# The recurrent stage of a four-layer graph kernel: 512 columns per matmul instead of 256, PSUM shared by two streams, straight-line code

## The chip, the cores and the metric

One core of a Trainium2 chip runs the whole program. The time is that of the device for one execution, in microseconds (us). The core has five engines that run side by side and meet at semaphores: TensorE (PE in the profile; PEld is its weight load), VectorE (DVE), ScalarE (ACT), GpSimd (POOL) and SyncE (SP, which issues the transfers between memory and SBUF). TensorE writes only to PSUM, which has 8 banks of 512 fp32 values in each of 128 partitions.

## The reference, cut to what matters

The input x is [128 graphs, 64 nodes, 256 features], and each of four layers computes `x = layernorm(x + layer(x))`. Layer 0 is a spectral convolution with attention and an MLP. Layer 1 is two graph convolutions followed by four small LSTMs, and it is the one that the change is in. Layer 2 is a graph convolution with two batch norms. Layer 3 is a masked attention. The part of layer 1 that matters here:

```python
def _lstm_last(Wih, Whh, bih, bhh, xs):          # xs [N, p, 256]
    bias = bih + bhh
    def step(carry, x_t):
        h, c = carry
        g = x_t @ Wih.T + h @ Whh.T + bias       # 1024 gate columns
        i, f, gg, o = jnp.split(g, 4, axis=-1)
        c = sigmoid(f) * c + sigmoid(i) * tanh(gg)
        h = sigmoid(o) * tanh(c)
        return ((h, c), None)
    ...                                          # h and c start at zero
for p in range(1, 5):                            # "skip" p
    nw = 64 // p
    wins = h[:, :nw * p, :].reshape(128 * nw, p, 256)
    last = _lstm_last(Wih[p-1], Whh[p-1], bih[p-1], bhh[p-1], wins)
    h = h.at[:, arange(nw) * p + p - 1, :].set(last)
```

For skip p there are 128 x (64 // p) windows, and each goes through p steps one after the other. In the first step h and c are zero, so neither Whh nor the forget gate is needed there. Skip p+1 reads what skip p has written.

## The kernel before, in words

The state `H` lies in SBUF with the 256 features on the partitions (two blocks of 128, `KD` = 2) and the 8192 tokens along the free side. Matrix products that must be exact to nearly fp32 are done by `exact_mm` (line 295): each operand is split into a rounded high part and a low rest (both fp32r), and three matmuls (high x high, low x high, high x low) accumulate. So a gate half (128 of the 1024 gate columns) costs 2 x 3 = 6 matmuls in a window's first step and 12 in a later one. A first step has three gates (36 matmuls), a later step four (96).

The recurrent stage (lines 1041 to 1252) runs two streams, s = 0 and 1 (`LS` = 2). Each takes a chunk of graphs so that a step has 256 columns (`COLS`): 4, 8, 12 and 16 graphs for skips 1 to 4 (for skip 3, 252 of the 256 columns hold data, and 84 in the last chunk of each stream, but all 256 are streamed). The order on each engine is: skip, turn, step j, stream. PE does one step of stream 0, then one of stream 1, and so on. Each stream has four PSUM banks of its own, one for each gate; a bank holds both halves of 256 columns (`gate_ps`, line 1112).

One step goes like this. PE waits for the split input `xin[s]` and for `hid_ready[s]` (the stream's previous step is wholly done), and does the gates in the order input, candidate, forget, output. ACT takes each gate out of PSUM with sigmoid or tanh (line 1155, two instructions per gate), and after the last gate takes the tanh of the cell (line 1160). DVE computes the cell (lines 1201 to 1207) and the new h (line 1212), and splits h into `hin[s]` (lines 1214 and 1216); in a window's last step it writes to `H` instead (line 1219). Then ACT and DVE split the input of the stream's next step (lines 1146 and 1189). While they do this, PE does the other stream's step.

The turns of a skip are a loop (`Fori`) whose last turn or two are written out. At the start of each skip, ACT and DVE split the new weights into the single weight buffer `w_r` (lines 1142 and 1180) and the inputs of both streams' first steps, which need the whole of the skip before. The raw weights come by DMA into staging areas in `H2`. Those of layer 2 are split at the start of the next stage (lines 1342 and 1369), whose first PE work is line 1407 and whose first DVE work is line 1377.

Of the kernel before, what the change touches and what calls it, by code (L numbers as in the profile page):

```python
# [121 lines left out]
def build_program(nc, ctx, t, out_rows):  # L122
# [23 lines left out]
    H2 = sb("H2", [P, KD, BATCH, NODES])  # L146
    Hflat = H[:].rearrange("p k b n -> p k (b n)")
    H2flat = H2[:].rearrange("p k b n -> p k (b n)")
# [42 lines left out]
    sm_inv = sb("sm_inv", [P, STREAMS, 2 * NJ])  # L191

# [47 lines left out]
    st = region(H2_words[:, 2 * 4096:])  # L240
    lstm_stage = [[st(KD, GATES * D), st(KD, GATES * D)] for _ in range(2)]
    l2r = region(H2_words[:, 2 * 4096:])
    l2_raw = [l2r(KD, HID2), l2r(MB, D)]
# [4 lines left out]
    W3_WORDS = 3 * KD * ATT3 + 2 * D  # L248

# [39 lines left out]
    def raw(v):  # L289

        return v.bitcast(F32)
# [15 lines left out]
    lstm_loaded = [sem(f"lstm_loaded{p}") for p in range(MAX_SKIP)]  # L307
    l2_loaded = sem("l2_loaded")
# [330 lines left out]
    with nc.Block() as block:  # L639

        @block.sync
        def _(sp):
# [19 lines left out]
            sp.dma_start(lstm_stage[0][0], t["wih"][0]).then_inc(lstm_loaded[0], 16)  # L662
# [270 lines left out]
    with nc.Block() as block:  # L933

        @block.sync
        def _(sp):
            for s in S:
                sp.dma_start(xg_t[s], rows_of_group(state0, s, 0)).then_inc(xg_loaded[s], 16)
            sp.dma_start(lstm_stage[1][0], t["wih"][1]).then_inc(lstm_loaded[1], 16)
            sp.dma_start(lstm_stage[1][1], t["whh"][1]).then_inc(lstm_loaded[1], 16)  # L940
# [101 lines left out]
    COLS = 256  # L1042
    lb = region(H2_words[:, 0:2 * 4096])
    gate = [lb(GATES, KD * COLS) for _ in range(LS)]
    cell = [lb(KD * COLS) for _ in range(LS)]
    hid = [lb(KD * COLS) for _ in range(LS)]
    lr = region(R[:])
    w_r = lr(2, 2, KD, GATES * D)
    xin = [lr(2, KD, COLS) for _ in range(LS)]
    hin = [lr(2, KD, COLS) for _ in range(LS)]  # L1050
    order = (0, 2, 1, 3)

    def gates_of(j):
        return [q for q in order if not (q == 1 and j == 0)]

    class Skip:

        def __init__(self, p):
            self.p = p  # L1060
            self.nw = NODES // p
            self.nb = COLS // self.nw
            self.turns = -(-BATCH // (self.nb * LS))
            self.nb_last = (BATCH - self.nb * LS * (self.turns - 1)) // LS
            self.per_turn = sum(len(gates_of(j)) for j in range(p))
            self.stage = lstm_stage[(p - 1) % 2]
            self.parts = [(w, k) for w in range(1 if p == 1 else 2) for k in range(KD)]
            self.gates_done, self.act_done = sems(f"gates_done{p}_", LS), sems(f"act_done{p}_", LS)
            self.x_hi, self.x_ready = sems(f"x_hi{p}_", LS), sems(f"x_ready{p}_", LS)
            self.cell_ready, self.tanh_ready = sems(f"cell_ready{p}_", LS), sems(f"tanh_ready{p}_", LS)  # L1070
            self.hid_ready, self.steps = sems(f"hid_ready{p}_", LS), sems(f"lstm_steps{p}_", LS)
            self.w_hi, self.w_ready = psem(f"w_hi{p}"), psem(f"w_ready{p}")

        def graphs(self, turn):
            return self.nb_last if isinstance(turn, int) and turn == self.turns - 1 else self.nb

        def window(self, turn, s, j):

            n = self.graphs(turn)
            last = isinstance(turn, int) and turn == self.turns - 1  # L1080
            first = (self.turns - 1) * LS * self.nb + s * n if last else (turn * LS + s) * self.nb
            return H[:, :, bass.ds(first, n), j:j + self.p * (self.nw - 1) + 1:self.p]

        def as_window(self, v, turn):

            n = self.graphs(turn)
            return v[:, :, 0:n * self.nw].rearrange("p k (b w) -> p k b w", b=n)

        def run(self, eng, step):

            looped = self.turns - 1 if self.nb_last == self.nb else self.turns - 2
            with eng.Fori(0, looped) as i:
                for j in range(self.p):
                    for s in range(LS):
                        step(i, j, s, (i, j + 1) if j < self.p - 1 else (i + 1, 0))
            for turn in range(looped, self.turns):
                for j in range(self.p):
                    for s in range(LS):
                        after = (turn + 1, 0) if turn < self.turns - 1 else None
                        step(turn, j, s, (turn, j + 1) if j < self.p - 1 else after)  # L1100

        def wait_for_all(self, eng):

            for s in range(LS):
                eng.wait_ge(self.hid_ready[s], self.turns * self.p + 1)

    skips = [Skip(p) for p in range(1, MAX_SKIP + 1)]

    def blocks_at(q, s):
        return blocks_of(gate[s][:, q, :])  # L1110

    def gate_ps(s, q, m):
        b = q * KD + m
        return ps[:, 4 * s + b // 2, (b % 2) * COLS:(b % 2 + 1) * COLS]

    with nc.Block() as block:

        @block.sync
        def _(sp):
            for skip in skips:  # L1120
                p, parts = skip.p, skip.parts
                if p in (1, 2):
                    sp.wait_ge(skip.w_ready, len(parts))
                    sp.dma_start(lstm_stage[(p + 1) % 2][0], t["wih"][p + 1]).then_inc(lstm_loaded[p + 1], 16)
                    sp.dma_start(lstm_stage[(p + 1) % 2][1], t["whh"][p + 1]).then_inc(lstm_loaded[p + 1], 16)
                if p == 3:
                    sp.wait_ge(skip.w_ready, len(parts))
                    sp.dma_start(l2_raw[0], t["L2W1"]).then_inc(l2_loaded, 16)
                    sp.dma_start(l2_raw[1], t["L2W2"]).then_inc(l2_loaded, 16)
                    for dst, name in ((Wq3, "Wq3"), (Wk3, "Wk3"), (Wv3, "Wv3"), (Wo3, "Wo3")):  # L1130
                        sp.dma_start(dst, t[name]).then_inc(l3_loaded, 16)
                    sp.dma_start(bo3, rows("bo3")).then_inc(l3_loaded, 16)

        @block.scalar
        def _(act):
            for skip in skips:
                p, parts = skip.p, skip.parts
                act.wait_ge(lstm_loaded[p - 1], 16 if p == 1 else 32)

                def split_weights(parts):  # L1140
                    for w, k in parts:
                        act.activation(w_r[:, 0, w, k, :], skip.stage[w][:, k, :], ACT.Copy).then_inc(skip.w_hi, 1)

                def split_x(s, turn, j):

                    act.activation(skip.as_window(xin[s][:, 0], turn), skip.window(turn, s, j), ACT.Copy)\  # L1146
                       .then_inc(skip.x_hi[s], 1)

                def step(turn, j, s, nxt):
                    done = sum(len(gates_of(jj)) for jj in range(j))  # L1150
                    act.wait_ge(skip.hid_ready[s], turn * p + j + 1)
                    for n, q in enumerate(gates_of(j)):
                        act.wait_ge(skip.gates_done[s], turn * skip.per_turn + done + n + 1)
                        for m in range(KD):
                            ins = act.activation(blocks_at(q, s)[:, m, :], gate_ps(s, q, m),  # L1155
                                                 ACT.Tanh if q == 2 else ACT.Sigmoid,
                                                 bias=lstm_bias[:, p - 1, 2 * q + m:2 * q + m + 1])
                        ins.then_inc(skip.act_done[s], 1)
                    act.wait_ge(skip.cell_ready[s], turn * p + j + 1)
                    act.activation(blocks_at(2, s), blocks_of(cell[s]), ACT.Tanh).then_inc(skip.tanh_ready[s], 1)  # L1160
                    if nxt:
                        split_x(s, *nxt)

                split_weights(parts[:KD])
                if p > 1:
                    skips[p - 2].wait_for_all(act)
                for s in range(LS):
                    split_x(s, 0, 0)
                split_weights(parts[KD:])
                skip.run(act, step)  # L1170

# [639 lines left out]
```

## Time and profile before

| what | value |
|---|---|
| median of 3 runs | 2538.29 us (2537.64 to 2539.34) |
| profiled execution, span from first to last instruction | 2536.9 us |
| PE busy | 2313.9 us, 91% |
| DVE busy | 1616.9 us, 64% |
| ACT busy | 1306.8 us, 52% |
| mean granted TensorE clock | 0.977 |
| recurrent stage, first to last matmul | about 904.3 to 1962.5 us |

The profile gives no time for its own execution other than the span. The median of the runs is 1.4 us above it, and that difference is taken as what lies around the span. Busy time on PE is the union of the matmul records, whose ends are modelled. A matmul's record is longer than its spacing from the next, so the spacing is read from counts over a busy stretch and not from the mean duration.

### The profile page before, as it was taken

The page shows a single profiled execution, that of the slowest core. Times are in us where ns is not written, and L with a number is a line of the kernel's source. Part 1 is how long each engine was busy: PE and PEld are TensorE (multiplying, and loading weights), DVE is VectorE, ACT ScalarE, POOL GpSimd, SP SyncE. Part 2 cuts the span into 40 slices and gives each one's busy share as a digit, 9 for nine tenths or more (in the row PEclk, how much of TensorE's full clock was granted, in tenths as well). Part 3 has the DMA queues.
Part 4 walks back from the last instruction along what each step waited for, and adds up shares of the span by engine and source line. Part 5 has one row for each costly group of instructions (what it writes and reads, how often), then busy time and mean ns, then how long its engine had stood idle before and what let it go on. Part 6 is the DMA issues. An engine that isn't in the chain of part 4 may idle for free. (4 is left out here: it accounts for less than half of the span.)

```text
span 2536.9 us, 48069 instructions
## 1 busy us (share of the span) xinstructions
PE 2313.9 (91%) x17943; PEld 2195.9 (87%) x17943; DVE 1616.9 (64%) x3379; ACT 1306.8 (52%) x2645; POOL 496.5 (20%) x937
## 2 busy tenths in 40 slices
PE   5989998999969999999999999999999897968887
PEld 4888888888869999999999999999999897956665
DVE  4898889888955544444444443444443787858887
ACT  1343344334423379755554444444443666957775
POOL 3334433433430000000000000000000221035554
PEclk9999999999989999999999999999999898989998
DMA  3010011011121100000000000000000331012111
GB/s 98 22 51 29 30 41 50 21 34 44 34 100 50 49 33 0 34 0 0 0 28 1 0 0 1 1 1 0 0 0 1 116 116 34 0 38 67 58 59 45
DMA packets 76385, 81.59 MB, mean 32 GB/s; under 512 B 6545, under 2 KB 74001, under 8 KB 75409
## 3 DMA queue, kind: packets, MB, share of 16 engines
q1 hardware_dynamic: 76304, 80.51, 10.1%
q8 instruction: 51, 0.84, 0.1%
q14 instruction: 30, 0.24, 0.0%
HBM read 55.33 MB, written 25.17 MB: 32 GB/s over the span
## 5 line engine op out<-in xcount | busy, mean ns | idle before, releaser
L298 PE MATMUL ps<-R 128*128 128x256 f32 x12816 | 1586.0, 285 | 56.5 <-DVE R L1189 22.6
L298 PEld LDWEIGHTS ps<-R 128*128 128x128 f32 x12816 | 1558.6, 193 | 68.0 <-DVE R L748 24.3
L1155 ACT ACTIVATE H<-ps,lstm_bias 128x256 f32<-128x256 f32 x920 | 380.8, 474 | 491.0 <-PE ps L298 490.7
L341 POOL TENSOR_TENSOR ln_veps<-ln_mv,eps_tile 128x2 f32<-128x2 f32 x128 | 29.1, 227 | 1388.6 <-DVE ln_mv L324 1388.6
L823 PE MATMUL ps<-H 128*128 128x256 f32 x1024 | 237.8, 381 | 3.0 <-ACT H L730 1.7
L823 PEld LDWEIGHTS ps<-H 128*128 128x128 f32 x1024 | 188.9, 191 | 26.2 <-ACT H L730 1.9
L1203 DVE TENSOR_TENSOR H<-H 128x512 f32<-128x512 f32 x64 | 44.4, 693 | 182.7 <-ACT H L1155 182.7
L320 DVE BATCH_NORM_STATS2 ln_stats<-H 128x6 f32<-128x256 f32 x384 | 144.2, 417 | 7.5 <-POOL H L695 2.0
L1205 DVE TENSOR_TENSOR H<-H 128x512 f32<-128x512 f32 x64 | 44.4, 693 | 139.9 <-ACT H L1155 139.9
L1219 DVE TENSOR_TENSOR H<-H 128x512 f32 (+4 forms) x68 | 51.3, 755 | 110.5 <-ACT H L1160 110.5
L352 ACT ACTIVATE H<-H,ln_shift,ln_rstd 128x256 f32<-128x256 f32 x192 | 104.0, 590 | 18.4 <-POOL ln_shift L346 18.4
L367 DVE SCALAR_TENSOR_TENSOR H<-H,ln_rstd 128x256 f32<-128x256 f32 x192 | 108.4, 606 | 6.9 <-POOL ln_rstd L334 3.2
L1212 DVE TENSOR_TENSOR H<-H 128x512 f32<-128x512 f32 x64 | 44.3, 693 | 100.8 <-ACT H L1160 100.8
L1146 ACT ACTIVATE R<-H 128x512 fp32r (+4 forms) x132 | 108.0, 822 | 0.0
L1189 DVE TENSOR_TENSOR R<-H,R 128x512 fp32r<-128x512 f32 (+2 forms) x132 | 106.4, 809 | 0.4
L344 POOL TENSOR_TENSOR ln_rstd<-ln_veps,minus_half 128x2 f32<-128x2 f32 x128 | 93.3, 729 | 10.0
L362 DVE SCALAR_TENSOR_TENSOR H<-H,ln_mv 128x256 f32<-128x256 f32 x192 | 89.0, 504 | 2.8 <-issue 1.6
L1201 DVE TENSOR_TENSOR H<-H 128x512 f32<-128x512 f32 x68 | 46.9, 690 | 63.0 <-ACT H L1155 62.8
L730 ACT ACTIVATE H<-ps,b_col 128x256 f32<-128x256 f32 x128 | 50.2, 474 | 71.1 <-PE ps L298 71.1
L1160 ACT ACTIVATE H<-H 128x512 f32<-128x512 f32 x132 | 83.1, 630 | 0.4
L1006 PE MATMUL ps<-adjT,H 128*128 128x128 f32 x512 | 61.0, 281 | 20.1 <-DMA H<-residual 20.1
L1006 PEld LDWEIGHTS ps<-adjT,H 128*128 128x128 f32 x512 | 60.3, 198 | 20.5 <-issue 20.5
(206 smaller groups left out, 2966.8 us busy)
## 6 DMA issues: line engine op xcount, KB each, us to landing
H<-in_x SPq DMA_DIRECT2D x64, 256.0 KB, 4.1
H<-residual SPq DMA_DIRECT2D x64, 256.0 KB, 2.8
residual<-H SPq DMA_DIRECT2D x32, 256.0 KB, 2.2
arena<-residual SPq DMA_DIRECT2D x32, 256.0 KB, 2.7
residual<-arena SPq DMA_DIRECT2D x32, 256.0 KB, 2.2
out<-H SPq DMA_DIRECT2D x32, 256.0 KB, 2.2
H<-in_wih SPq DMA_DIRECT2D x4, 1024.0 KB, 4.9
H<-in_whh SPq DMA_DIRECT2D x3, 1024.0 KB, 7.3
```

What stands on the lines that cost most here:

```text
L298: mm = pe.matmul(out, lhsT(a), rhs(b), start=start and n == 0, stop=stop and n == len(PASSES) - 1)
L320: c.step(dve.bn_stats(ln_stats[:, s, n, :], y[:, n, :]))
L344: c.step(pool.tensor_tensor(ln_rstd[:, s, :], ln_veps[:, s, :], minus_half[:, 0:TILES], ALU.pow))
L352: ins = act.activation(y[:, n, :], y[:, n, :], ACT.Identity, bias=ln_shift[:, s, n:n + 1], scale=ln_rstd[:, s, n:n + 1])
L362: c.step(dve.scalar_tensor_tensor(out=y[:, n, :], in0=y[:, n, :], scalar=ln_mv[:, s, n, 0:1], in1=g, op0=ALU.subtract, op1=ALU.mult))
L367: ins = dve.scalar_tensor_tensor(out=y[:, n, :], in0=y[:, n, :], scalar=ln_rstd[:, s, n:n + 1], in1=be, op0=ALU.mult, op1=ALU.add)
L823: mm = pe.matmul(out[:, n, :], src[:, k, n * P:(n + 1) * P], w[:, k, :], start=(k == 0), stop=(k == blocks - 1))
L1006: mm = pe.matmul(out[:, k, n * P:(n + 1) * P], src[:, n, k * P:(k + 1) * P], adjT[:], start=True, stop=True)
L1146: act.activation(skip.as_window(xin[s][:, 0], turn), skip.window(turn, s, j), ACT.Copy)\
L1155: ins = act.activation(blocks_at(q, s)[:, m, :], gate_ps(s, q, m), ACT.Tanh if q == 2 else ACT.Sigmoid, bias=lstm_bias[:, p - 1, 2 * q + m ...
L1160: act.activation(blocks_at(2, s), blocks_of(cell[s]), ACT.Tanh).then_inc(skip.tanh_ready[s], 1)
L1189: dve.tensor_tensor(skip.as_window(xin[s][:, 1], turn), skip.window(turn, s, j), skip.as_window(raw(xin[s][:, 0]), turn), ALU.subtract)\
```

## The change

Each step now has 512 columns, as graphs per chunk: 8 for skip 1, 16 for skip 2, 22 (four chunks) and 20 (two chunks) for skip 3, and 32 for skip 4. Step widths are exact: a chunk of 22 graphs has 462 columns and one of 20 has 420. A gate's half fills one PSUM bank, so the eight banks hold the four gates once, for both streams together. Before PE writes a gate, it waits until ACT has taken the same gate of the step before (the other stream's) out of its banks.

The whole stage is written out with no loop. ACT takes the tanh of the cell ahead of the output gate. The tanh gate and the forget gate share one buffer, so ACT waits for the product of input and candidate gate before it writes the forget gate. The first half of `H2` becomes fp32r inputs (`R2`) and the second half work buffers (`late_half`).

The weights have six slots instead of one buffer, and stage through two areas in the arena. ACT and DVE split them between steps (`SPLIT_AFTER`), two pieces at a time, those of layer 2 too. For skips 3 and 4 the recurrent matrix Whh is split after the skip's own first step. The input of a skip's first step waits only for the chunks of the skip before that cover its graphs (`outputs_needed`).

The core of the diff:

```diff
     LS = 2
-    COLS = 256
...
+    COLS = 512
...
+    wslot = [lr(2, GATES * D) for _ in range(6)]
...
+    MATRICES = (("wih", 0, (0, 1)), ("whh", 1, (2, 3)), ("wih", 1, (4, 5)), ("wih", 2, (0, 1)),
+                ("whh", 2, (4, 5)), ("wih", 3, (2, 3)), ("whh", 3, (0, 1)))
...
+    CHUNKS = {1: [8] * 16, 2: [16] * 8, 3: [22] * 4 + [20] * 2, 4: [32] * 4}
...
-    def gate_ps(s, q, m):
-        b = q * KD + m
-        return ps[:, 4 * s + b // 2, (b % 2) * COLS:(b % 2 + 1) * COLS]
...
+    def gate_ps(q, m, cols):
+        return ps[:, KD * q + m, 0:cols]
...
+    FIRST_OF = {p: next(n for n, x in enumerate(steps_l) if x.p == p) for p in range(1, MAX_SKIP + 1)}
+    SPLIT_AFTER = {}
+    for n, after in enumerate((FIRST_OF[1] + 2, FIRST_OF[1] + 6, FIRST_OF[2] + 2, FIRST_OF[3], FIRST_OF[3] + 4,
+                               FIRST_OF[4], FIRST_OF[4] + 4), 1):
+        for k in range(KD):
+            SPLIT_AFTER.setdefault(after, []).append((n, k))
...
         @block.scalar
         def _(act):
...
+                for a, q in enumerate(x.gates):
+                    if q == SIGM_F:
+                        act.wait_ge(ig_ready[s], sum(1 for y in steps_l[:n + 1] if y.s == s and y.j))
+                    if q == SIGM_O:
+                        act.wait_ge(cell_ready[s], x.nth + 1)
+                        act.activation(x.part(bg), x.part(cell[s]), ACT.Tanh).then_inc(tanh_ready[s], 1)
+                    act.wait_ge(gates_done[s], gb + a + 1)
+                    for m in range(KD):
+                        ins = act.activation(into[q][:, m, 0:x.cols], gate_ps(q, m, x.cols),
+                                             ACT.Tanh if q == TANH_G else ACT.Sigmoid,
+                                             bias=lstm_bias[:, x.p - 1, 2 * q + m:2 * q + m + 1])
+                    ins.then_inc(act_done[s], 1)
+                if n + LS < len(steps_l):
+                    split_x(steps_l[n + LS])
+                for w, k in SPLIT_AFTER.get(n, ()):
+                    split_weights(w, k)
...
         @block.tensor
         def _(pe):
...
+            for n, x in enumerate(steps_l):
+                s, before = x.s, steps_l[n - 1] if n else None
+                pe.wait_ge(w_ready, READY["whh" if x.j else "wih", x.p - 1])
+                pe.wait_ge(x_ready[s], x.nth + 1)
+                if x.j:
+                    pe.wait_ge(hid_ready[s], x.nth)
+                operands = [("wih", xin, k) for k in range(KD)] + [("whh", hin, k) for k in range(KD) if x.j]
+                for q in x.gates:
+                    if before and q in before.gates:
+                        pe.wait_ge(act_done[before.s], before.gates_before + before.gates.index(q) + 1)
+                    for m in range(KD):
+                        f = slice((q * KD + m) * P, (q * KD + m + 1) * P)
+                        for a, (name, src, k) in enumerate(operands):
+                            w = wslot[SLOTS[name, x.p - 1][k]]
+                            mm = exact_mm(pe, gate_ps(q, m, x.cols), lambda h: w[:, h, f],
+                                          lambda h: src[s][:, h, k, 0:x.cols], a == 0, a == len(operands) - 1)
+                    mm.then_inc(gates_done[s], 1)
```

How the instructions stand. On PE, the end of skip 3 and the whole of skip 4 stood like this before (128x256 is the output of one matmul, `REGISTER_ALU` and the branches are the loop's):

```order
L1092 UNCONDITIONAL_BRANCH
L1092 ISA
L298 MATMUL ps<-R 128x256 x72
L1240 REGISTER_ALU
L298 MATMUL ps<-R 128x256 x192
L1240 REGISTER_ALU
L298 MATMUL ps<-R 128x256 x192
L1240 REGISTER_ALU
L298 MATMUL ps<-R 128x256 x192
L1092 REGISTER_ALU
L1092 COMPARE_AND_BRANCH
L298 MATMUL ps<-R 128x256 x648
```

And the whole stage on PE now:

```order
L1237 UNCONDITIONAL_BRANCH
L298 MATMUL ps<-R 128x512 x1632
L298 MATMUL ps<-R 128x462 x912
L298 MATMUL ps<-R 128x420 x456
L298 MATMUL ps<-R 128x512 x1296
L1132 UNCONDITIONAL_BRANCH
```

The stage had 8592 executed matmuls of 256 columns; it now has 1632 + 1296 = 2928 of 512 columns, 912 of 462 and 456 of 420, which makes 4296.

On ACT, at the end of skip 1, one step of each stream and the start of skip 2 stood like this before (L1155 takes gates out of PSUM, L1160 is the tanh of the cell, L1142 splits weights, L1146 inputs):

```order
L1155 ACTIVATE H<-ps,lstm_bias 128x256 x6
L1160 ACTIVATE H<-H 128x512
L1155 ACTIVATE H<-ps,lstm_bias 128x256 x6
L1160 ACTIVATE H<-H 128x512
L1142 ACTIVATE R<-H 128x1024 x2
L1146 ACTIVATE R<-H 128x512 x2
L1142 ACTIVATE R<-H 128x1024 x2
```

Now, in skip 1 (L1179 takes gates out of PSUM, L1176 is the tanh of the cell, L1159 splits the next input):

```order
L1179 ACTIVATE late_half<-ps,lstm_bias 128x512 x4
L1176 ACTIVATE late_half<-late_half 128x1024
L1179 ACTIVATE late_half<-ps,lstm_bias 128x512 x2
L1159 ACTIVATE R<-H 128x1024
L1179 ACTIVATE late_half<-ps,lstm_bias 128x512 x4
```

The tanh has moved ahead of the last gate, and the split of an input follows each step.

On DVE, the change from skip 2 to skip 3 before (L1219 writes a result to `H`, L1180 splits weights, L1189 inputs, L1201 is the first cell product of skip 3):

```order
L1219 TENSOR_TENSOR H<-H 128x2x256
L1180 TENSOR_TENSOR R<-H,R 128x1024 x2
L1189 TENSOR_TENSOR R<-H,R 128x2x252 x2
L1180 TENSOR_TENSOR R<-H,R 128x1024 x2
L1092 UNCONDITIONAL_BRANCH
L1092 ISA
L1201 TENSOR_TENSOR H<-H 128x512
```

And now (L1223 writes a result, L1198 splits an input, L1212 is the cell product, L1226 to L1230 make and split h, L1193 splits weights):

```order
L1223 TENSOR_TENSOR H<-late_half 128x2x512
L1198 TENSOR_TENSOR R<-H,R 128x2x462
L1212 TENSOR_TENSOR late_half<-late_half 128x2x462
L1226 TENSOR_TENSOR late_half<-late_half 128x2x462
L1228 TENSOR_SCALAR R<-late_half 128x2x462
L1230 TENSOR_TENSOR R<-late_half,R 128x2x462
L1198 TENSOR_TENSOR R<-H,R 128x2x462
L1193 TENSOR_TENSOR R<-arena,R 128x1024 x2
L1212 TENSOR_TENSOR late_half<-late_half 128x2x462
```

No weight split stands between the skips any more; Whh of skip 3 is split after the first step's own work.

## Rows read from the trace of the kernel before

**Rows 1.** The page: span, and busy time, share, instructions by engine.
```profile
span 2536.9 us, 48069 instructions
PE 2313.9 (91%) x17943; PEld 2195.9 (87%) x17943; DVE 1616.9 (64%) x3379; ACT 1306.8 (52%) x2645; POOL 496.5 (20%) x937
```
**Rows 2.** Stretches of line 298, skips 1 to 4: us, PE and PEld busy (x), clock, DMA.
```profile
904.30:1044.40 140.10, 140.09 (x1152) 140.09 (x1152) 0.98 0.04 15
1050.10:1305.80 255.70, 255.65 (x2111) 255.65 (x2112) 0.99 0.02 8
1311.60:1641.80 330.20, 330.16 (x2736) 329.95 (x2736) 1.00 0.02 6
1647.80:1962.60 314.80, 314.40 (x2592) 313.41 (x2592) 0.99 0.00 1
```
**Rows 3.** Who waited for whom, 899 to 1975: us in total, times, longest.
```profile
ACT H L1155 <- PE ps L298: 490.7, 338, 2.7
PE ps L298 <- DVE R L1189: 22.6, 4, 5.8
```
**Rows 4.** PE in four stretches: us, busy (x), granted clock, DMA share, GB/s.
```profile
1051.00:1055.00 4.00, 4.00 (x20) 0.50 0.25 49
1320.00:1640.00 320.00, 320.00 (x2665) 1.00 0.00 1
...
1895.00:1960.00 65.00, 65.00 (x544) 1.00 0.00 1
```
**Rows 5.** Durations, ns min/median/max, of lines 298 and 823 on PE.
```profile
L298 PE MATMUL ps<-R x12816: 274/283/583, 54.8 to 2229.7; 128*128 128x256 f32 x198
L823 PE MATMUL ps<-H x1024: 377/379/793, 44.1 to 726.3; 128*128 128x256 f32 x171
```
**Rows 6.** The page's costliest groups: busy, mean ns, idle before and its releaser.
```profile
L298 PEld LDWEIGHTS ps<-R 128*128 128x128 f32 x12816 | 1558.6, 193 | 68.0 <-DVE R L748 24.3
L823 PE MATMUL ps<-H 128*128 128x256 f32 x1024 | 237.8, 381 | 3.0 <-ACT H L730 1.7
L823 PEld LDWEIGHTS ps<-H 128*128 128x128 f32 x1024 | 188.9, 191 | 26.2 <-ACT H L730 1.9
```
**Rows 7.** The same groups by shape, 899 to 1966: ACT and DVE.
```profile
L1155 ACT ACTIVATE H<-ps,lstm_bias 128x256 f32<-128x256 f32 x920 | 380.8, 474 | 491.0 <-PE ps L298 490.7
...
L1201 DVE TENSOR_TENSOR H<-H 128x512 f32<-128x512 f32 x68 | 46.9, 690 | 63.0 <-ACT H L1155 62.8
L1180 DVE TENSOR_TENSOR R<-H,R 128x1024 fp32r<-128x1024 f32 x14 | 16.5, 1226 | 6.2 <-ACT R L1142 6.2
L1142 ACT ACTIVATE R<-H 128x1024 fp32r<-128x1024 f32 x14 | 14.0, 1052 | 1.0 <-PEq L142 1.0
```
**Rows 8.** By shape elsewhere: strided inputs of skips 3, 4, and a 1024-wide scalar operation.
```profile
L1189 DVE TENSOR_TENSOR R<-H,R 128x504 fp32r<-128x504 f32 x28 | 23.9, 854 | 0.2
L1189 DVE TENSOR_TENSOR R<-H,R 128x512 fp32r<-128x512 f32 x30 | 32.8, 1093 | 0.2
L1486 DVE TENSOR_SCALAR R<-arena 128x1024 fp32r<-128x1024 f32 x32 | 22.2, 694 | 12.0 <-ACT arena L1463 11.9
```
**Rows 9.** In order of time, start of the stage: start us, us, instruction [idle before].
```profile
903.57 1.29 DVE L1189 TENSOR_TENSOR R<-H,R 128x512 fp32r<-128x512 f32 x2
904.32 7.87 PE L298 MATMUL ps<-R 128*128 128x256 f32 x48 [5.76 <-DVE R L1189]
```
**Rows 10.** In order of time, end of the stage and start of the next.
```profile
1957.83 4.72 PE L298 MATMUL ps<-R 128*128 128x256 f32 x38
...
1962.59 0.84 ACT L1155 ACTIVATE H<-ps,lstm_bias 128x256 f32<-128x256 f32 x2 [2.04 <-PE ps L298]
...
1964.05 1.06 DVE L1219 TENSOR_TENSOR H<-H 128x512 f32<-128x512 f32 x1 [2.04 <-ACT H L1160]
1966.25 1.92 SPq L1310 DMA_DIRECT2D arena<-residual  x4
...
1972.62 0.69 DVE L1377 TENSOR_TENSOR arena<-ps,arena 128x512 f32<-128x512 f32 x1 [2.89 <-DMA arena<-residual]
```

More of the change, by code:

```diff
@@ L236, in build_program @@
     bg1 = wg(D)
[L240 to L243, printed above, removed]
     w3 = region(arena[:])
@@ L248, in build_program @@
     W3_WORDS = 3 * KD * ATT3 + 2 * D
+    st = region(arena[:, W3_WORDS:])
+    wstage = [st(KD, GATES * D) for _ in range(2)]
     def tiles_of(v):
@@ L1041, in build_program @@
     LS = 2
-    COLS = 256
[L1043 to L1046, printed above, removed]
-    lr = region(R[:])
[L1048 to L1051, printed above, removed]
-    def gates_of(j):
[L1054 to L1105, printed above, removed]
@@ L1107, in build_program @@
-    skips = [Skip(p) for p in range(1, MAX_SKIP + 1)]
-    def blocks_at(q, s):
-        return blocks_of(gate[s][:, q, :])
-    def gate_ps(s, q, m):
-        b = q * KD + m
-        return ps[:, 4 * s + b // 2, (b % 2) * COLS:(b % 2 + 1) * COLS]
+    COLS = 512
+    upper.close()
+    upper = ExitStack()
+    R2 = upper.enter_context(nc.sbuf_tensor("R2", [P, STATE_WORDS // 2], F32R))
+    late_half = upper.enter_context(nc.sbuf_tensor("late_half", [P, STATE_WORDS // 2], F32))
+    lb = region(late_half[:])
@@ new lines, in build_program, with __init__, window, as_window @@
+    CHUNKS = {1: [8] * 16, 2: [16] * 8, 3: [22] * 4 + [20] * 2, 4: [32] * 4}
+    class Step:
+        def __init__(self, p, c, j, nth, gates_before):
+            self.p, self.c, self.j, self.s = p, c, j, c % LS
+            self.nth, self.gates_before = nth, gates_before
+            self.last = j == p - 1
+            self.graphs, self.nw = CHUNKS[p][c], NODES // p
+            self.first = sum(CHUNKS[p][:c])
+            self.cols = self.graphs * self.nw
+            self.gates = gates_of(j)
+        def window(self):
+            return H[:, :, self.first:self.first + self.graphs,
+                     self.j:self.j + self.p * (self.nw - 1) + 1:self.p]
+        def as_window(self, v):
+            return v[:, :, 0:self.cols].rearrange("p k (b w) -> p k b w", b=self.graphs)
+        def part(self, v):
+            return v[:, :, 0:self.cols]
@@ new lines, in build_program, with outputs_needed @@
+    steps_l = []
+    for p in range(1, MAX_SKIP + 1):
+        for c in range(0, len(CHUNKS[p]), LS):
+            for j in range(p):
+                for s in range(LS):
+                    mine = [x for x in steps_l if x.s == s]
+                    steps_l.append(Step(p, c + s, j, len(mine), sum(len(x.gates) for x in mine)))
+    def outputs_needed(step):
+        need = {}
+        for x in steps_l:
+            if x.p == step.p - 1 and x.last and x.first < step.first + step.graphs:
+                need[x.s] = max(need.get(x.s, 0), x.nth + 1)
+        return need
@@ new lines, in gate_ps @@
+    def gate_ps(q, m, cols):
[6 more added lines that the diff above has]
+            SPLIT_AFTER.setdefault(after, []).append((n, k))
+    (gates_done, act_done, ig_ready, cell_ready, tanh_ready, hid_ready, x_hi, x_ready, dve_steps) = (
+        sems("lstm_" + n, LS) for n in ("gates", "act", "ig", "cell", "tanh", "hid", "xhi", "xr", "dve"))
@@ L1119, in _ @@
         def _(sp):
[L1120 to L1132, printed above, removed]
+            for dst, name in ((Wq3, "Wq3"), (Wk3, "Wk3"), (Wv3, "Wv3"), (Wo3, "Wo3")):
+                sp.dma_start(dst, t[name]).then_inc(l3_loaded, 16)
@@ L1134, in _ @@
         @block.scalar
         def _(act):
[L1136 to L1170, printed above, removed]
```

192 lines of the change are left out of this document (103 added, 89 removed).

## The prediction

> **What bounds the kernel now.** I read the page's busy times first, then stretches of time, waits, durations, and the order of time at the two ends of the stage. PE is busy 91% of the span, DVE 64%, ACT 52% [rows 1]. In the recurrent stage it is plainer. Line 298 fills all four stretches, one for each skip, to within 0.4 us, and the stage is these stretches with three gaps between them of 5.7, 5.8 and 6.0 us: 904.3 to 1962.6, 1058.3 us [rows 2]. ACT waits 490.7 us for PE there, while PE waits for DVE only four times, at most 5.8 us, before a skip's first matmul [rows 3]. So the stage is PE's to set, and a change in ACT or DVE matters only where it shows up as a wait of PE.
>
> In a steady stretch 2665 matmuls of 256 columns take 320.0 us, 0.120 us each, at the full granted clock (2.4 GHz) [rows 4]. So 8592 take 1031.0 us. The four stretches hold 1040.2 us of busy PE [rows 2]; the other 9.2 us are matmuls after the four long waits at the low clock (1.2 GHz: 20 in 4.0 us [rows 4]) and short waits, at most 2.3 us a time.
>
> **Matmuls, the large term.** 256 columns at 2.4 GHz are 106.7 ns, yet the spacing is 120. The weights are changed before each matmul, and PEld is as busy as PE throughout [rows 2]. What does a matmul with twice the streaming cost? No fp32r matmul of 512 columns is in the trace. The nearest is line 823, a plain fp32 product whose records each stream 256 columns twice. Records overrun the spacing: line 298 has a median of 283 for a spacing of 120, so 163 ns are tail, and line 823 with 379 has a spacing of 216 [rows 5]. That is 512 / 2.4 = 213.3 plus 2.6, with a weight load of the same 0.19 us record between every two, and PEld idle a fifth of the time PE is busy (188.9 against 237.8) [rows 6]. I take this: the surplus of 13.3 ns comes from a load that only just fits beside 256 columns, and it vanishes when there are 512 to hide it.
>
> The bounds of one 512-column matmul: 213.3 ns below (pure streaming), 240 above (twice 120, the surplus goes with the columns); between them 226.7 (the surplus is one per matmul). I take 216, and for 462 and 420 columns 195 and 178 (2.6 plus columns / 2.4). The sum is 2928 x 0.216 + 912 x 0.195 + 456 x 0.178 = 632.4 + 177.8 + 81.2 = 891.4 us, instead of 1031.0. Of the 139.6 saved, 36.5 are columns of skip 3 no longer streamed (8592 x 256 = 2,199,552 columns against 2,112,000), which no theory disputes.
>
> The Trainium skill, "TensorE: Matmul & The Clock Gate", section Back-to-back issue gap, gives columns / 2.4 plus 2.5 ns for a matmul by itself. For line 823 the trace agrees (216), for line 298 not (120, the rule says 109). By the rule alone the stage would have had 940 us of matmuls before, and halving their number would be worth 11 us beside the columns; the rows have the larger surplus, and the sum goes by them.
>
> **Between the skips.** The 17.5 us of gaps go: no weight or input split stands there, and the inputs need only early chunks. Three of four slow-clock spells go with them; the first stays, 2.3 us. What is late next is the chain of a first step (j = 0) of stream 0, since only the other stream's first step, 36 x 0.216 = 7.8 us, covers it. With 0 where PE leaves the step, for 512 columns: the candidate gate was done at -2.6, ACT starts 0.2 later (as at the stage's end, matmul record until 1962.55 less its tail, ACT at 1962.59 [rows 10]) and a pair of activations takes 1.2 (0.84 for 256 columns [rows 10], plus twice 256 columns at the 0.75 ns that lie between 474 and 1052 [rows 7]): until -1.2. DVE's cell product, 1.23, until 0.1. The tanh, 1.05 as line 1142, until 1.2. The output gate until 2.4. DVE's h, 1.23, its rounding, 0.69 [rows 8], its rest, 1.23 [rows 7]: until 5.6. The next input's split, 1.2 in skip 2, about 1.5 in skip 3 (854 ns for 504 [rows 8]), 2.0 in skip 4 (1093 for 512 [rows 8]): 6.8, 6.6 (all is a tenth shorter with 462 columns) and 7.6, plus some 0.25 for the hand-overs. PE comes at 7.8, 7.0 and 7.8. So skips 2 and 3 wait for nothing and skip 4 about 0.2.
>
> But Whh of skips 3 and 4 is split after that chain, two pieces of 1.2 us on DVE, and PE's second step waits for it: 6.85 + 2.4 against 7.0 is 2.2 us, 7.85 + 2.4 against 7.8 is 2.4 us. Behind the waiting PE stand only the rest of its own matmuls; ACT and DVE then have a step of 96 x 0.216 = 20.7 us to catch up. Both waits: between 0 and twice 5.8. With the other pair of skip 4, 4.8 us. Whether the clock falls after a wait of 2.4 us no row shows; 0 to 2.3 us each, and I take 0.
>
> The pieces for other skips cost nothing: they lie beside skip 1 steps, where PE has 7.8 us and DVE 3.7 for a step (three operations of 1.23), 6.2 with the pieces. ACT has 3 x 1.2 + 1.05 + 1.05 = 5.7 us. If that cover were gone, each of the two such places would cost at most 2.4 us. The new wait for a shared bank costs nothing either: the same gate of the step before was finished by PE a whole step earlier less one gate, 5.2 us or more, and ACT needs 1.4 to 2.5.
>
> **Ends.** At the start DVE's first input split is 1.23 instead of a 0.69 us piece (two take 1.29 [rows 9]): 0.5 us later. At the end the output gate's pair is 1.2 instead of 0.84 and the strided write about 2.0 instead of 1.06 [rows 10], the tanh between them having moved ahead (0.4): 0.9 later. Layer 2's weight split no longer leads its stage, but line 1377 waits there for the residual rows, issued at 1966.25 and used at 1972.62 [rows 10]. That transfer hides the split: gain 0, 3.5 us if it doesn't. The straight-line code: PE already ran a written-out part, 1895 to 1960, at 544 matmuls in 65 us without idling [rows 4], so I charge nothing.
>
> **The sum.** Stage after: 891.4 + 2.3 + 4.8 = 898.5, against 1058.3: 159.8 less. Less 0.5 and 0.9: 158.4. The profiled span 2536.9 becomes 2378.5, and with the 1.4 that the runs' median lies above the span, 2379.9.
>
> **Rivals.**
> A, the surplus is one per matmul: 4296 x 13.3 = 57.1 in place of 11.2, less 1 us of shorter waits: 2425. For it: it is what a fixed cost would look like at 256 columns. Against: line 823 doesn't have it, and at the low clock 20 matmuls in 4.0 us leave no room for more than 256 / 1.2 = 213 ns of streaming each.
> B, it goes with the columns, a rate of 4-byte operands: 2,112,000 x 0.46875 ns = 990.0, less 2 of waits: 2476. For it: nothing but that line 823 is no fp32r product. It too is hidden at the low clock.
> C, slower: PE halts at the gates for the shared banks, and each halt keeps the clock at 1.2 GHz, where a 512-column matmul takes 427 ns. If half of the work ran so, 891.4 / 2 = 446 more: 2826. It decides from 158.4 / 891.4 = 18% of the work. For it: the clock did fall at every long wait. Against: the steady stretches with waits under half a us hold 0.99 to 1.00 [rows 2], and the waits for banks come out at none. The Trainium skill, the same page, section A second HAM failure mode, tells of just this at 512 columns with PSUM banks cycled, small idles between groups and a clock that swings; no row here has it.
> D, the chain is 2 us longer than worked out, in all nine places (4 + 3 + 2 chunk pairs of skips 2 to 4): at most 18 more, 2398. For it: skip 4 has no slack left. Against: every link of it is a row.
>
> **How the numbers follow.** Forecast 58%, A 20%, B 12%, D 6%, C 4%. The likeliest's own range is 2366 (no waits for Whh, layer 2's split gained, 213.3 ns) to 2392 (both waits longer, slow clock after them). To leave out no more than 2 in 10 the whole range reaches over A and D: 2366 to 2436; B is outside. A measurement here tells some 0.2% (5 us) from no change: faster 95% (forecast, A, B, D), within 0.2% 1%, slower 4% (C).
>
> **What would show it.** Matmuls of 512 columns at 216 ns in a steady stretch (right), 227 (A), 240 (B); the three gaps gone; two waits of PE of 2 to 3 us at the second step of skips 3 and 4; PEld visibly less busy than PE; clock 0.99 or more. It would be wrong if PE idled at the gates, or if line 1377 came earlier after the stage's end.

## The result: 2433.9 us, 4.1% less, and the profile after

| | before | after |
|---|---|---|
| median of 4 runs | 2537.97 us (2537.05 to 2539.34) | 2433.86 us (2432.31 to 2434.57) |
| ratio, 95% interval | | 0.9588, 0.9575 to 0.9602 |
| span of the profiled execution | 2536.9 us | 2432.8 us |
| recurrent stage, first to last matmul | 904.3 to 1962.5: 1058.2 us | 906.1 to 1856.4: 950.3 us |

The forecast was 2380, with a range of 2366 to 2436. The time is inside, 2.1 us under the top, and nearest to rival A (2425). The forecast promised 158 us less and 104 came. The forecast's own range, 2366 to 2392, is missed; the stated one holds the time only because it was stretched to take in A.

The page after, the lines that answer to [rows 1]:

```profile
span 2432.8 us, 37529 instructions
PE 2220.7 (91%) x13647; PEld 1966.1 (81%) x13647; DVE 1561.0 (64%) x3053; ACT 1181.5 (49%) x2039; POOL 496.7 (20%) x937
```

PEld's share fell from 87% to 81% while PE's stayed at 91%: the weight load now has room. Three steady stretches of line 298 after, in skips 2, 3 and 4 (us, PE busy (x), PEld busy (x), granted clock, DMA share, GB/s), answer to [rows 2, 4]:

```profile
1060.00:1270.00 210.00, 210.00 (x929) 173.92 (x928) 1.00 0.02 6
1310.00:1470.00 160.00, 160.00 (x758) 142.68 (x757) 1.00 0.02 7
1600.00:1850.00 250.00, 250.00 (x1105) 207.01 (x1104) 1.00 0.00 1
```

250 us hold 1105 records, those at both borders included, and the steps between records are 227 or 226 ns: 226.7 for a matmul of 512 columns. It is not 216. PE doesn't idle and the clock is at its full level (2.4 GHz), so each matmul itself is longer than forecast. Who waited for whom in the stage after, against [rows 3]:

```profile
PE ps L298 <- DVE R L1198: 6.4, 1, 6.4
PE ps L298 <- DVE R L1193: 2.5, 2, 1.5
```

One wait is the stage's start. The other two, 1.0 and 1.5 us, are for the weight split (L1193), at the second steps of skips 3 and 4. The three gaps between skips are gone, and no wait for a shared bank appears.

The groups of line 298 within the stage, by shape (busy us, mean ns, idle before):

```profile
L298 PEld LDWEIGHTS ps<-R 128*128 128x128 f32 x4296 | 808.3, 188 | 148.1 <-issue 6.5 <-DVE R L1193 3.4
L298 PE MATMUL ps<-R 128*128 128x512 f32 x2928 | 666.5, 390 | 7.9 <-DVE R L1198 6.4 <-DVE R L1193 1.5
L298 PE MATMUL ps<-R 128*128 128x462 f32 x912 | 193.5, 374 | 1.0 <-DVE R L1193 1.0
L298 PE MATMUL ps<-R 128*128 128x420 f32 x456 | 88.3, 354 | 0.0
```

They give 212 ns for 462 columns (193.5 / 912) and 193.6 for 420. The mean 390 less the 163 ns of tail is 227, the same reading that gave 216 for line 823 [rows 5].

Where the 104.1 us of the span came from, by these rows:

| part | forecast | measured |
|---|---|---|
| matmuls at the full clock: 1031.0 before, now | 891.4 | 663.8 + 193.3 + 88.3 = 945.4 |
| gaps between skips (17.5) | -17.5 | -17.5 |
| slow clock and short waits: 9.2 before, now | 2.3 | 947.7 busy - 945.4 = 2.3 |
| waits for Whh, chain of skip 4 | +4.8 | +2.5 |
| before the stage's first matmul | +0.5 | +1.8 |
| after its last | +0.9 | +2.1 |

The 947.7 is PE's busy time over the whole stage, 906.1 to 1856.4, where the records of two widths that overlap count once. The measured column adds up to 103.6 of the 104.1; the rest is 0.5 us of idle inside the four stretches before.

### The profile page after: what moved, and what is told of

It is laid out like the page before. It is cut to its first block and busy times, and to the rows that moved or that the text cites. A ratio compares the mean times of both kernels' runs of the same rounds, so it can differ in the third digit from the quotient of the medians.

```text
span 2432.8 us, 37529 instructions
## 1 busy us (share of the span) xinstructions
PE 2220.7 (91%) x13647; PEld 1966.1 (81%) x13647; DVE 1561.0 (64%) x3053; ACT 1181.5 (49%) x2039; POOL 496.7 (20%) x937
## 3 DMA queue, kind: packets, MB, share of 16 engines
q1 hardware_dynamic: 76304, 80.51, 10.7%
## 5 line engine op out<-in xcount | busy, mean ns | idle before, releaser
L298 PE MATMUL ps<-R 128*128 128x256 f32 (+3 forms) x8520 | 1493.0, 335 | 40.6 <-DVE R L747 17.3
L298 PEld LDWEIGHTS ps<-R 128*128 128x128 f32 x8520 | 1327.9, 190 | 189.8 <-DVE R L747 22.0
L1179 ACT ACTIVATE late_half<-ps,lstm_bias 128x512 f32<-128x512 f32 (+2 forms) x460 | 283.0, 669 | 383.3 <-PE ps L298 383.2
L1214 DVE TENSOR_TENSOR late_half<-late_half 128x1024 f32<-128x1024 f32 (+2 forms) x32 | 37.6, 1176 | 186.8 <-ACT late_half L1179 186.8
L1176 ACT ACTIVATE late_half<-late_half 128x1024 f32<-128x1024 f32 (+2 forms) x66 | 68.1, 1032 | 124.4 <-DVE late_half L1219 78.5
L1216 DVE TENSOR_TENSOR late_half<-late_half 128x1024 f32<-128x1024 f32 (+2 forms) x32 | 37.6, 1176 | 132.6 <-ACT late_half L1179 132.6
L1223 DVE TENSOR_TENSOR H<-late_half 128x1024 f32<-128x1024 f32 (+2 forms) x34 | 45.9, 1349 | 89.2 <-ACT late_half L1179 89.2
L319 DVE BATCH_NORM_STATS2 ln_stats<-H 128x6 f32<-128x256 f32 x256 | 96.0, 417 | 5.3 <-POOL H L694 2.0
L1198 DVE TENSOR_TENSOR R<-H,R 128x1024 fp32r<-128x1024 f32 (+2 forms) x66 | 95.7, 1452 | 1.3 <-ACT R L1159 1.1
L1159 ACT ACTIVATE R<-H 128x1024 fp32r<-128x1024 f32 (+2 forms) x66 | 94.4, 1431 | 0.0
L1226 DVE TENSOR_TENSOR late_half<-late_half 128x1024 f32<-128x1024 f32 (+2 forms) x32 | 37.6, 1176 | 81.1 <-ACT late_half L1179 81.1
L1212 DVE TENSOR_TENSOR late_half<-late_half 128x1024 f32<-128x1024 f32 (+2 forms) x34 | 40.9, 1202 | 58.6 <-ACT late_half L1179 58.5
L323 DVE BATCH_NORM_AGGREGATE ln_mv<-ln_stats 128x2 f32<-128x6 f32 x448 | 56.3, 166 | 33.7 <-DVE ln_stats L319 15.7
```

Of the source, the lines that this page charges most:

```text
L298: mm = pe.matmul(out, lhsT(a), rhs(b), start=start and n == 0, stop=stop and n == len(PASSES) - 1)
L319: c.step(dve.bn_stats(ln_stats[:, s, n, :], y[:, n, :]))
L323: ins = dve.bn_aggr(ln_mv[:, s, n, :], ln_stats[:, s, n, :])
L1159: act.activation(x.as_window(xin[x.s][:, 0]), x.window(), ACT.Copy).then_inc(x_hi[x.s], 1)
L1176: act.activation(x.part(bg), x.part(cell[s]), ACT.Tanh).then_inc(tanh_ready[s], 1)
L1179: ins = act.activation(into[q][:, m, 0:x.cols], gate_ps(q, m, x.cols), ACT.Tanh if q == TANH_G else ACT.Sigmoid, bias=lstm_bias[:, x.p - 1 ...
```

## The experiments

Two theories stood for the surplus over columns / 2.4 GHz. L, the forecast's: the weight load just fits beside 256 columns and the surplus goes at 512. F: each fp32r matmul has a fixed price of 13.3 ns, whatever its width (this is rival A of the prediction).

**Matmuls alone.** One line per kind, for example:

```diff
+ for n in range(N):
+     pe.matmul(ps[:, n // 12 % 8, 0:512], w(wr, n), xr[:, 0, 0:512], start=n % 12 == 0, stop=n % 12 == 11)
```

> All of the reference's computation is left out: the kernel runs rows of 48 matmuls on TensorE and nothing beside them, one row per line, weights changed before each unless said. What is asked is where the 13.3 ns come from by which an fp32r matmul's spacing exceeds columns / 2.4 GHz, at 256 columns (120 ns) as at 512 (226.7 ns). Theory F (a fixed price of each fp32r matmul): 226.7 at 512 columns on every line (same or changed weights, one or two inputs, long groups or single ones, 128 or 64 weight columns), 173.3 at 384, 120 at 256, bf16 at 512 without it (about 216). Theory L (the weight load): 64 weight columns bring 512 and 256 columns near columns / 2.4 + 2.6, and so does bf16. Theory P (PSUM groups or changing inputs in the real kernel): the first line, with one input, long groups and nothing beside it, is at 216. Widths 504, 480, 464, 462, 448, 420: theory F has columns / 2.4 + 13.3 for all (195.9 + 9.9 = 205.8 for 462, 188.3 for 420); the changed kernel showed 212 and 194 there, and if widths that are no multiple of 16 or 32 cost more, 448, 464 and 480 are on the formula and 462 and 420 some 6 above it.

The lines' records: duration min/median/max in ns, then the us at which the line's first and last matmul start; the spacing is their difference over 47. These times are rounded to 0.1 us; the spacings below are those of the unrounded records.

```profile
L60 PE MATMUL ps<-xr,wr x48: 388/390/390, 24.2 to 34.9; 128*128 128x512 f32 x48
L66 PE MATMUL ps<-xr,wr x48: 387/392/398, 56.9 to 67.7; 128*64 128x512 f32 x48
L68 PE MATMUL ps<-xr,wr x48: 333/335/347, 67.9 to 76.1; 128*128 128x384 f32 x48
L70 PE MATMUL ps<-xr,wr x48: 278/284/284, 76.3 to 81.9; 128*128 128x256 f32 x48
L86 PE MATMUL ps<-xb,wb x48: 272/273/273, 152.5 to 157.7; 128*128 128x256 bf16 x48
L88 PE MATMUL ps<-xf,wf x48: 379/380/381, 157.8 to 167.9; 128*128 128x256 f32 x48
```

fp32r has 227, 174 and 120 ns at 512, 384 and 256 columns: 13 to 14 above the streaming (columns / 2.4) each time. The same 227 stands with one weight for all 48 matmuls and with single groups in changing banks (L62 and L64 have the median of L60, 390). The last line, with one input and long groups, has it too, so theory P is out. bf16 at 256 columns has 109, 2.5 above. And the length of the weight load is not it: with 64 weight columns (L66) its mean record falls to 135 ns from 188, and the spacing rises to 230.

```profile
L66 PEld LDWEIGHTS ps<-xr,wr 128*64 128x64 f32 x48 | 6.5, 135 | 4.5
```

So F, and L is out. Two things stay open. Every line loads weights before each matmul, the line with one weight too (48 loads), so a price for having any load between two fp32r matmuls isn't told apart from a price of the matmul. And no line of 256 columns has 64 weight columns: that 256 pays the same price rests on 384 here, and on 320 in the next run. L88 shows what misled me. A record of plain fp32 with 256 columns has 216, as line 823 did, but it is another kind of matmul, which doesn't pay the price. (Its 24 matmuls left 48 records, so such a matmul takes two of these steps.) Not all of F's numbers held: 504 columns have the 227 of 512, 480 have 217 (213.3 by F), 464 have 209 (206.7), 448 have 203 (200), and 462 have 212 (205.8), more than 464. With 420, at 187 (188.3), the price over these widths is 12 to 19 ns.

**A second row of them.**

```diff
+ for n in range(N):
+     pe.matmul(ps[:, n // 12 % 8, 0:512], w(wr if n % 2 else wb, n), (xr if n % 2 else xb)[:, 0, 0:512], ...)
```

> Again only rows of 48 matmuls with all else of the reference left out. The first such run had 226.7 ns for fp32r at 512 columns whatever the weights and groups, and 216 for bf16. Asked: is the price in the switch of the instruction or in each fp32r matmul, and where does the weight load take over below 256 columns? Theory F (13.3 ns per fp32r matmul): alternating fp32r and bf16 at 512 columns gives a mean of (226.7 + 216) / 2 = 221; 64 rows of weights and inputs in place of 128 give 226.7 all the same; 320 columns 146.7; at 224, 210, 192 and 128 columns the spacing leaves columns / 2.4 + 13.3 for a floor of 107 to 113 ns, the weight load's (210 columns showed 112 in the kernel with 256-column steps). Rival (fp32r reads its inputs slower by a share, 13.3 at 512 and at 256 being two different things): 64 rows or alternation change the price. Widths 510, 462, 456, 440, 420 with the input alternating between two halves of the buffer: by the kernel's trace 462 has 212 to 214 and 420 194, above the formula's 205.8 and 188.3.

```profile
L60 PE MATMUL ps<-xr,wr x48: 383/386/493, 24.5 to 35.3; 64*128 64x512 f32 x48
L62 PE MATMUL ps<-xr,wr x24: 578/578/581, 35.6 to 46.2; 128*128 128x512 f32 x24
L64 PE MATMUL ps<-xr,wr x48: 218/275/277, 46.6 to 51.8; 128*128 128x128 f32 x48
L70 PE MATMUL ps<-xr,wr x48: 272/274/281, 62.7 to 68.0; 128*128 128x224 f32 x48
L76 PE MATMUL ps<-xr,wr x48: 350/354/354, 80.7 to 89.8; 128*128 128x420 f32 x48
L82 PE MATMUL ps<-xr,wr x48: 365/373/382, 109.6 to 119.6; 128*128 128x462 f32 x48
```

With 64 rows (L60) the median duration less the tail is 223, and the common step is 227: F. 320 columns have 147, again F. Alternating kinds (L62) take 10.6 us for 46 steps, 230 each, not the 221 that I expected, so a change of kind costs as well. Below 256 columns there is a floor: 128 and 224 columns both have 111 to 113 ns, and 256 columns lie just above it. That the floor is the weight load is argued and not shown, since no line so narrow has a shorter load of this kind; bf16 at 128 columns has 56. With the input alternating between halves, 462 columns have 212 and 420 have 193, as in the kernel, and 6 and 5 above F. With one input 462 had 212 as well, but 420 had 187. Why such widths cost more stays open.

**256 columns again, all else as changed.**

```diff
-    COLS = 512
+    COLS = 256
-    CHUNKS = {1: [8] * 16, 2: [16] * 8, 3: [22] * 4 + [20] * 2, 4: [32] * 4}
+    CHUNKS = {1: [4] * 32, 2: [8] * 16, 3: [12] * 4 + [10] * 8, 4: [16] * 8}
```

> The changed kernel with 256 columns per step again (4, 8, 12 or 10, and 16 graphs), all else as changed: shared banks, straight-line code, weights between steps, exact widths in skip 3 (252 and 210 columns). Theory F (a fixed price of 13.3 ns of each matmul, and the rest of the change costs nothing): 5856 matmuls of 256 at 120 ns, 912 of 252 and 1824 of 210 at columns / 2.4 + 13.3 or 6 more: 702.7 + 109 + 185 = 997 and up to 16 more, against 948.3 now: 2434 + 49 to 65 = 2483 to 2499 us. Theory L (the weight load is a floor of 120 ns): the 2736 narrow ones are at 120 too: 1031, and 2434 + 83 = 2517. If shared banks or the chain of a first step (4.3 us of cover now) bind, PE shows waits of 0.3 us or more at the gates or steps, and the time is above 2517.

It took 2505.1 us (2504.4 to 2508.3), ratio to before 0.9868 (0.9853 to 0.9883). F had 2483 to 2499 and L 2517; neither holds alone, because the floor does count for the 1824 matmuls of 210 columns, 112 ns (203.9 / 1824) where F has 101, and because PE waited 5.0 us for two weight splits, now with half the cover, and 1.3 for banks:

```profile
L298 PE MATMUL ps<-R 128*128 128x256 f32 x5856 | 708.8, 284 | 10.7 <-DVE R L1198 5.8 <-DVE R L1193 2.6 <-ACT late_half L1179 1.3
L298 PE MATMUL ps<-R 128*128 128x210 f32 x1824 | 203.9, 274 | 0.0
L298 PE MATMUL ps<-R 128*128 128x252 f32 x912 | 107.0, 280 | 2.6 <-DVE R L1193 2.4 <-issue 0.2
```

This run splits the change in two: the width is worth 2505.1 - 2433.9 = 71 us, and everything else, with the exact widths of skip 3, 34 (2538.9 before on this chip, less 2505.1). The 71 hold 3.8 us of waits more than the changed kernel has, and skip 3's floor.

**Skip 3 at its full width.**

```diff
+                cols = COLS if x.p == 3 else x.cols
...
-                                          lambda h: src[s][:, h, k, 0:x.cols], a == 0, ...)
+                                          lambda h: src[s][:, h, k, 0:cols], a == 0, ...)
```

> The changed kernel, but skip 3 streams 512 columns per matmul and not 462 or 420 (the rest are stale values that nothing reads), which undoes the exact widths. By the spacings in the changed kernel's trace (226.7, 212 and 193.6 ns) it costs 912 x 14.7 + 456 x 33.1 = 28.5 us: 2462. If the extra 6 ns of the narrow widths were not tied to the width but to skip 3's place in the program, the skip would have 232.7 ns and the time would be 2470. If streamed columns were free (some other bound), 2434.

It took 2460.8 us (2459.5 to 2461.7), 26.9 more than the changed kernel, where 28.5 was expected. In the profiled executions the stage itself is 29.0 longer (904.3 to 1883.6), though the wait for Whh in skip 3 shrank from 1.0 to 0.3. The difference lies outside it: the stage starts 1.8 earlier here, and 1.7 less lies behind it, both in code that the edit doesn't touch. All 4296 matmuls of the stage have the same step of 226.7 ns:

```profile
1310.00:1590.00 280.00, 280.00 (x1237) 231.85 (x1236) 1.00 0.01 4
```

So the odd surplus of skip 3 belongs to the widths, and not streaming dead columns is a quarter of the whole gain: 27 us, where the prediction had 36.5 "which no theory disputes".

**The split of Whh one step earlier.**

```diff
-    ... (FIRST_OF[1] + 2, FIRST_OF[1] + 6, FIRST_OF[2] + 2, FIRST_OF[3], FIRST_OF[3] + 4,
-         FIRST_OF[4], FIRST_OF[4] + 4)
+    ... (FIRST_OF[1] + 2, FIRST_OF[1] + 6, FIRST_OF[2] + 2, FIRST_OF[3] - 1, FIRST_OF[3] + 4,
+         FIRST_OF[4] - 1, FIRST_OF[4] + 4)
```

> The changed kernel with the split of Whh of skips 3 and 4 one step earlier: after the last step of the skip before, not after the skip's own first step. My theory of the two waits (1.4 and 1.9 us in the changed kernel's trace, before the second step of skips 3 and 4: the split stands behind the first step's chain on VectorE) expects them gone or under 0.5 us, since VectorE has room there, and 2 to 3 us less: 2431.5. The rival (the chain itself is late, the split only stands beside it) expects the waits to stay at over 1 us each and the time within 1 us of 2433.9.

In the changed kernel, in order of time at the second step of skip 3 (start us, us, instruction, idle before):

```profile
1289.76 1.12 DVE L1230 TENSOR_TENSOR R<-late_half,R 128x924 fp32r<-128x924 f32 x1
...
1290.80 1.43 DVE L1198 TENSOR_TENSOR R<-H,R 128x924 fp32r<-128x924 f32 x1
...
1292.14 2.35 DVE L1193 TENSOR_TENSOR R<-arena,R 128x1024 fp32r<-128x1024 f32 x2
...
1294.55 3.65 PE L298 MATMUL ps<-R 128*128 128x462 f32 x16 [1.02 <-DVE R L1193]
```

The input was ready at 1292.2, before PE was free at 1293.5; the weights at 1294.5. (The 1.4 and 1.9 us of the expectation are PEld's waits at these two places; PE's are 1.0 and 1.5.) With the split a step earlier DVE has it behind it before the chain begins, and PE runs through:

```profile
1279.80 16.45 PE L298 MATMUL ps<-R 128*128 128x462 f32 x77
...
1280.69 2.35 DVE L1193 TENSOR_TENSOR R<-arena,R 128x1024 fp32r<-128x1024 f32 x2
...
1283.34 1.12 DVE L1212 TENSOR_TENSOR late_half<-late_half 128x924 f32<-128x924 f32 x1 [0.30 <-ACT late_half L1179]
```

Both waits are gone, as the theory had it. The time, 2428.6 us (2426.1 to 2431.2), is 5.2 less, where 2 to 3 were expected. The rest is not shown to be the edit's: the profiled execution had its first matmul of the stage 1.3 us earlier than the changed kernel's, ahead of anything edited, and the 456 matmuls of 420 columns took 191 ns each (87.3 us in all) where they had 193 (88.3):

```profile
L298 PE MATMUL ps<-R 128*128 128x420 f32 x456 | 87.3, 354 | 0.0
```

The next two versions have the same 87.3. The inputs lie where they lay, so their place alone doesn't set the price of this width.

**The loads at the start of layer 2.** There the changed kernel's trace has lost time, against [rows 10]:

```profile
1860.54 1.92 SPq L1315 DMA_DIRECT2D arena<-residual  x4
...
1868.27 0.69 DVE L1375 TENSOR_TENSOR arena<-ps,arena 128x512 f32<-128x512 f32 x1 [8.52 <-DMA arena<-residual]
```

7.7 us pass from the first issue to the first use, where it was 6.4 before. Three other runs have the same loads in the same order there, and 7.0 (256 columns), 6.7 (Whh earlier) and 5.9 (skip 3 at full width): the 1.3 us lie within what executions differ by. The edit here, on top of the earlier split:

```diff
-            for s in S:
+            for s in reversed(S):
                 sp.dma_start(ys_t[s], rows_of_group(state0, s, 0)).then_inc(ys_loaded[s], 16)
```

> The kernel with the earlier Whh split (2428.6 us), and at the start of layer 2 the four loads of the residual rows are issued in the order of streams 3, 2, 1, 0 and not 0 to 3. In the changed kernel VectorE's first work there (line 1375) waits until 7.7 us after the first of the four is issued, and the last of them lands just then; in the order of the work stream 3 comes first. Theory: it waits for the load issued last, so the reversal lets it start some 3.5 to 4 us after the first issue, when TensorE's transposes are there: 4 us less, 2424.6. Rival: the delay is VectorE's own (its code arriving at the start of the stage, 16 KB fetched in 1.2 us just then): nothing gained, 2428.6.

```profile
1855.61 3.23 SPq L1315 DMA_DIRECT2D arena<-residual  x4
1857.07 2.82 PE L1404 MATMUL ps<-ident,arena 128*128 128x128 f32 x12 [5.63 <-ACT arena L1351]
1860.26 0.69 DVE L1375 TENSOR_TENSOR arena<-ps,arena 128x512 f32<-128x512 f32 x1 [5.44 <-DMA arena<-residual]
```

It took 2426.3 us (2423.5 to 2428.3). DVE starts 4.65 us after the first issue, 3.1 sooner than in the changed kernel and 2.0 sooner than in the run that this one is built on. It had waited for the load issued last: in the changed kernel that load was issued at 1862.0 and took 6.2 us to land, and DVE started at 1868.27. The times of this run and the last overlap, 2.3 between medians, so the gain is seen in the trace and not told apart by the times.

**All first loads.** This stands on top of the two edits before.

```diff
-            sp.dma_start(wstage[0], t["wih"][0]).then_inc(stage_loaded[0], 16)     # end of layer 0
...
-            for s in S:
+            for s in reversed(S):                                                  # layers 1, 2 and 3
...
+            sp.dma_start(wstage[0], t["wih"][0]).then_inc(stage_loaded[0], 16)     # layer 1, behind its rows
             sp.dma_start(wstage[1], t["whh"][1]).then_inc(stage_loaded[1], 16)
```

> As the run with the loads of layer 2 reversed, and the same reversal at the start of layers 1 and 3, and the 1 MB load of the first input weights issued after layer 1's first loads and not ahead of them. If these waits too are for the load issued last: in layer 1 TensorE starts at 3.5 us after the issue and not 6.4, in layer 3 VectorE some 3 us earlier: another 5 to 6 us, 2419. If at these places something else comes last (the write of the rows, the code), as the run before, 2424.6 or, where the other holds, 2428.6.

It took 2418.4 us (2418.0 to 2418.7), ratio to before 0.9528 (0.9515 to 0.9541), as the first theory had it (2419). At the start of layer 1 PE comes 3.0 us after the first issue, not 6.4; in layers 2 and 3 DVE comes 2.8 and 2.9 us after it, not 7.7 and 7.5; in layer 3 it then waits for PE and no longer for a load. In layer 2 nothing differs from the run before, which had 4.65, so one trace gives such a gain only to about 2 us. In layer 1 two edits stand together, the order and the 1 MB load behind the others, and their shares aren't told apart. In the changed kernel each of the four loads there took 4.3 us or more to land, so the order alone wouldn't have brought PE to 3.0:

```profile
740.47 1.92 SPq L936 DMA_DIRECT2D H<-residual  x4
...
743.49 5.24 PE L1004 MATMUL ps<-adjT,H 128*128 128x128 f32 x32 [16.28 <-DMA H<-residual]
```
```profile
1852.06 1.92 SPq L1315 DMA_DIRECT2D arena<-residual  x4
...
1854.81 0.69 DVE L1375 TENSOR_TENSOR arena<-ps,arena 128x512 f32<-128x512 f32 x1 [3.53 <-DMA arena<-residual]
```

This version beats both kernels, by 4.7% and 0.6%.

## Why the prediction was right, and where it was off

The time fell inside the range, but the forecast's main term was wrong, and what came was rival A, which had a chance of 20%.

The direction, the gaps, the shared banks, the straight-line code and the clock came as forecast. The term that was mis-sized is the 512-column matmul: 216 ns taken, 226.7 measured. That is 4296 x 10.7 = 46 of the 54 us between 891.4 and 945.4; the other 8 are the widths of skip 3, 212 and 193.6 instead of 195 and 178 (of which 13.3 - 2.6 are already counted).

The step that failed is "the surplus of 13.3 ns comes from a load that only just fits beside 256 columns". Two readings had the same number at 256 columns, a load of 107 ns with a hand-over and a fixed price of the kind, and I let line 823 decide. It has 512 column passes per record, but it is plain fp32, and the price belongs to fp32r (227 against 216 in the first run of matmuls alone). That the two differ in kind was in the text, as the weak case for rival B; it was as much a case for A. The low clock, which I held against A, doesn't speak: at 1.2 GHz the stage shows 213 and 427 ns, pure streaming, with the price in it hidden: the clock is 0.50 from 906.1 to 910.2, and the steps of 512 columns there are 426 or 427.

The chain of a first step was close: in skip 4 I had the input ready 7.85 us after PE left the step, where PE comes at 7.8. It was ready after 7.3 (1576.3). The matmuls being longer, PE came at 8.2 instead, and the waits for Whh were 1.0 and 1.5 in place of 2.2 and 2.4. The second pair of skip 4 didn't wait at all. Waits of this length left the clock at 1.00, so the 0 taken for it was right.

The start was 1.8 late where 0.5 was forecast: the last matmul before it is itself 1.1 later (it ends at 899.7 against 898.6). That isn't the change's: in the runs with other edits to the stage, whose code up to there is the same, this matmul ends between 897.9 and 899.3. From it to the first of the stage it is 6.4 us against 5.8: 0.6 more, near the 0.5 forecast. The end was 2.1 and not 0.9: layer 2's split was hidden by the transfer as said, but the transfer came later, within the 5.9 to 7.7 us that it took in the runs with the same loads. In the changed kernel one instruction fetch of 16 KB lies among these transfers; it lies there in those runs too, the one with 5.9 included, so it doesn't explain the 7.7.

Two sums of the prediction don't hold. The lower end of the forecast's own range, with no waits for Whh, layer 2's split gained and 213.3 ns, comes to 2360 and not 2366 (2379.9 - 4.8 - 3.5 - 11.2). And the 36.5 us for skip 3's columns are their streaming alone; the prices of 462 and 420 columns, higher than that of 512, took 8 of them.

Rival C, and with it the Trainium skill's "TensorE: Matmul & The Clock Gate", section A second HAM failure mode, found nothing here: 512 columns, eight banks cycled, and the granted clock is 1.00 in every steady stretch. PE had no idle between the groups but the two waits for Whh, so the case that the Trainium skill describes didn't arise. What the Trainium skill's same page gives under Back-to-back issue gap, columns / 2.4 plus 2.5 ns, holds for bf16 (109 at 256 columns, 216 at 512 by the steps of line 84) and for a record of plain fp32 (216), and not for fp32r.

## What to carry to other kernels

Fewer, wider matmuls save a fixed price each (here 13 ns), and the price must be read from a row of the same data type. When two mechanisms give one number, a row of another kind can't tell them apart. Don't stream columns that hold nothing: that was worth 27 of 104 us. At each stage's start, issue first the load that is used first: with the 1 MB load moved behind, that was worth 10 us over three starts (2428.6 to 2418.4).

## What the runs showed of the hardware

- From 128 to 224 columns an fp32r matmul with its weight load stays at 111 to 113 ns.
- Alternating fp32r and bf16 costs 230 ns each at 512 columns, more than the mean of the two (221).
- Between these widths the price is 12 to 19 ns, without a rule that the runs show: 504 columns have 227 as 512 have, 462 have 212 where 464 have 209, and 420 have 187, 191 or 193, the last two in kernels with the same place of the input.
- Of four loads of 256 KB issued together within 2 us, the one issued last landed 7.7 us after the first issue in one trace. Issued in the other order, the one needed first was there after 4.65 and 2.8 us.
